# Causal masks in attention on 64 by 64 cells of the array, each product writing one half of the rows

## What is computed

```python
scores = jnp.einsum('bthd,bshd->bhts', q, k) * scale
causal = jnp.tril(jnp.ones((S, S), dtype=bool))
scores = jnp.where(causal[None, None, :, :], scores, -jnp.inf)
probs = jax.nn.softmax(scores, axis=-1)
attended = jnp.einsum('bhts,bshd->bthd', probs, v).reshape(B, S, hidden)
return attended @ Wo.T + bo
```

## Time and profile before

| | |
|---|---|
| median of three runs | 1914.78 us |
| profiled execution | 1914.01 us |
| its span, first to last instruction | 1912.2 us |
| mean granted clock of TensorE, share of 2.4 GHz | 0.907 |
| busy: TensorE, VectorE, ScalarE, GpSimd | 87%, 62%, 49%, 27% of the span |
| MATMUL records | 13482 |

### The profile page before, as it was taken

How to read it: one execution, slowest core, us unless ns; L and a number is a source line. 1 busy time by engine, 2 the same in 40 slices (tenths; PEclk the granted TensorE clock), 3 DMA queues, 4 the chain that set the end, 5 groups by cost and what they waited for, 6 DMA issues and landing times. The chain is left out here.

```text
span 1912.2 us, 33758 instructions
## 1 busy us (share of the span) xinstructions
PE 1656.3 (87%) x13482; PEld 1086.1 (57%) x13482; DVE 1178.0 (62%) x1827; ACT 942.1 (49%) x1898; POOL 517.0 (27%) x401
## 2 busy tenths in 40 slices
PE   2665999999999979999956269999999997999998
PEld 2442455554554568888844235554545445888887
DVE  3545778878785366444464167778878816654444
ACT  1110487777778524334321006777777782444333
POOL 1114166556657512223222110000000000223222
PEclk7775799999999989999978657999999998999999
DMA  4331211112110060000006511020100004100000
GB/s 131 97 105 50 67 50 52 60 50 71 53 43 32 24 264 1 1 1 0 0 21 204 194 48 41 24 68 24 46 30 18 2 2 196 69 12 1 11 11 11
DMA packets 75992, 104.39 MB, mean 55 GB/s; under 512 B 28560, under 2 KB 46736, under 8 KB 75600
## 3 DMA queue, kind: packets, MB, share of 16 engines
q1 hardware_dynamic: 71888, 86.11, 14.0%
q0 software_dynamic: 3968, 16.39, 2.2%
HBM read 61.84 MB, written 40.37 MB: 53 GB/s over the span
## 5 line engine op out<-in xcount | busy, mean ns | idle before, releaser
L974 DVE TENSOR_REDUCE chunk_max<-ring 128x2 f32<-128x1024 f32 (+3 forms) x640 | 670.9, 1064 | 209.3 <-PE ring L881 104.5
L954 ACT ACTIVATE probs<-ps_s 128x512 f32<-128x512 f32 (+3 forms) x1280 | 620.0, 534 | 238.4 <-PE ps_s L911 153.5
L881 PE MATMUL ring<-kt,qt 63*128 63x512 f32 (+3 forms) x1280 | 465.1, 473 | 83.0 <-PEq L408 58.1
L906 PE MATMUL ps_s<-qt,kt 64*128 64x512 f32 (+3 forms) x1280 | 471.3, 437 | 5.2 <-ACT probs L954 4.5
L1245 POOL TENSOR_TENSOR inter_lo<-inter,inter_hi 128x512 fp32r<-128x512 f32 x128 | 165.5, 1293 | 936.3 <-ACT inter_hi L1179 936.3
L923 PE MATMUL ps_o<-probs,vg 128*32 128x256 f32 (+1 forms) x4608 | 360.5, 385 | 0.0
L906 PEld LDWEIGHTS ps_s<-qt,kt 64*128 64x128 f32 x1280 | 214.2, 190 | 239.1 <-ACT probs L954 204.6
L881 PEld LDWEIGHTS ring<-kt,qt 63*128 63x128 f32 x1280 | 206.5, 201 | 118.0 <-issue 59.2
L1219 DVE SCALAR_TENSOR_TENSOR gelu_a<-gelu_a,ps_g 128x512 f32<-128x512 f32 x128 | 88.0, 688 | 183.3 <-ACT gelu_a L1173 183.0
L1173 ACT ACTIVATE gelu_a<-ps_g 128x512 f32<-128x512 f32 x128 | 76.5, 598 | 228.8 <-PE ps_u L94 228.5
L92 PE MATMUL ps_d<-w_mlp,inter_lo 128*128 128x256 f32 x512 | 151.2, 295 | 28.8 <-DVE x L1210 15.2
(11 more groups left out here) (141 smaller groups left out, 2435.8 us busy)
## 6 DMA issues: line engine op xcount, KB each, us to landing
w_mlp<-w_scr SPq DMA_DIRECT2D x32, 768.0 KB, 15.3
w_scr<-w_parts POOLq DMA_DIRECT2D x16, 768.0 KB, 3.6
qt<-q_scr SPq DMA_DIRECT2D x116, 96.0 KB, 2.4
q_scr<-qk_hi SPq DMA_DIRECT2D x32, 256.0 KB
kt<-k_scr SPq DMA_DIRECT2D x80, 96.0 KB, 2.5
q_scr<-qk_lo SPq DMA_DIRECT2D x16, 256.0 KB
v_scr_b<-v_out SPq DMA_DIRECT2D x8, 512.0 KB, 10.3
k_scr<-qk_hi SPq DMA_DIRECT2D x16, 256.0 KB
```

The lines of the kernel that those rows point to most:

```text
L881: op = pe.matmul(out[:, h, 0:w], qt[g][plain[h], p, q0:q0 + P], kt[g][plain[h], p % NKP, c * TW:c * TW + w], start=True, stop=c < t)
L906: op = pe.matmul(out[:, 0:TW - w0], kt[g][shifted[h % 2], (h // 2) % NKP, kb * P:(kb + 1) * P], qt[g][shifted[h % 2], h // 2, t * TW + w0: ...
L954: act.activation(pr[n % NPR][:, h, w0:TW], src[:, 0:TW - w0], ACT.Exp, scale=SCALE).then_inc(s_e, 1)
L974: dve.tensor_reduce(mp[t % 2][:, qb, 2 * p:2 * p + 2, c], ring[n % 2][:, :, 0:w], AX.X, ALU.max).then_inc(s_rd, 1)
```

## The change

Each masking product is cut to the half of the output that it is about. Its weights are the 64 by 64 identity (`ident[half, 0, 0:64]`) for both a; the output is partitions 0 to 63 for a = 0 and 64 to 127 for a = 1; and of the 128 columns only those that can hold a masked value are written: from 64 a on above the diagonal, up to 64 (a + 1) below it. All else stays: the plan, the mask tiles, the semaphores.

```diff
                     if c == t:
                         for a in range(2):
-                            op = pe.matmul(out[:, h, w - P:w], ident[half[h], a, :], above[half[h], a, :],
-                                           start=False, stop=a == 1)
+                            c0 = HALF * a
+                            op = pe.matmul(out[half[a], h, w - P + c0:w], ident[half[h], 0, 0:HALF], above[half[h], a, c0:P],
+                                           start=False, stop=True)
...
                     if diagonal:
                         for a in range(2):
-                            op = pe.matmul(out[:, 0:P], ident[half[h % 2], a, :], below[half[h % 2], a, :],
-                                           start=False, stop=a == 1)
+                            c1 = HALF * (a + 1)
+                            op = pe.matmul(out[half[a], 0:c1], ident[half[h % 2], 0, 0:HALF], below[half[h % 2], a, 0:c1],
+                                           start=False, stop=True)
```

## The result

The changed kernel takes 2593.45 us (median of 4 runs, 2577.16 to 2608.27) against 1917.16 us before (4 runs on the same chip, 1914.37 to 1921.19): a ratio of 1.3523, 95% interval 1.3422 to 1.3625. It is slower by 676 us. The forecast was 2742 us with a range of 2010 to 2950. The profiled execution took 2603.55 us, its span 2601.7 us.

A forecast was written before the change was run, and what follows sets the result against it. TensorE was taken to bound the kernel in attention. Profiled execution 1914.0 us + 360 for waits at shape changes + 468 for the lower clock = 2742 us; its own range 2450 to 2950, overall range 2010 to 2950.

The forecast's parts named there:

- The wait: At each change between 64x128 and 64x64 cells in attention, the array runs empty: 0.095 us, bounds 0 to 0.095.
- All-masked stages: Between PV groups, stages with both scores and both maxima products masked: 2.28 us against some 0.85, 53 us per layer.
- main block: One score or maxima product with its exposed load, stream and wait: 0.435 us at 512 columns, 0.35 at 320.
- masked-S stage: Between PV groups, a stage with both scores S masked: 1.80 us against 0.78, 50 stages, 51 us per layer.
- mask block: One pair of masks: load 0.055, stream 0.07 and wait 0.095, together 0.22 us.
- my table: Sum over the attention stages by which products are masked: 180 us per layer, 360 for both, clock unchanged.
- The clock: TensorE falls to 1.2 GHz over 60% of attention, changed stages 1.6 times as long: 234 us per layer, 468 both.
- the dip of the earlier trace: Ground for the low clock: granted clock 0.50 at 1276.3, at a tile's change where the stream thins out.
- That the clock holds: Rival: in attention the waits come but the clock stays; 2274 us, say 2200 to 2400; chance 0.12.
- That there is no wait: Rival: no wait between 64x128 and 64x64 cells, pairs save 24 us; 1891 us, bounds 1842 to 1914; chance 0.15.
- only the mask's own half waits: Rival: M of the other row half keeps streaming, +0.11 us per pair, 113 us; 2027 us; chance 0.11.

The follow-up runs named there:

- held back: The changed kernel's 64x64 masks, kept in a list and issued together ahead of the next PV or a product that must not pass them: 1920.13 us.
- half in 64x64: The changed kernel, but only the a = 0 masking product has 64x64 cells, a = 1 stays 64x128, all bf16: 2624.66 us.
- M alone: Kernel before, with only the masks of the maxima products M cut to 64x64 cells, those of the scores S as before: 2025.32 us.
- S alone: Kernel before, with only the masks of the scores S cut to 64x64 cells, those of the maxima products M as before: 2429.53 us.
- its own control in 64x128 cells: Kernel before, with masks issued together ahead of PV, in 64x128 cells with only the needed columns: 1896.55 us, ratio 0.9896.

## Why the prediction was right, and where its sizes were off

**The bound.** TensorE was what a microsecond in attention would be paid in, and it was: 676 us more, VectorE's and ScalarE's instructions no longer than before and both waiting for TensorE.

**The wait.** Right, and shown: from a main product to its mask there are 0.42 and 0.43 us, and 0.31 behind an S whose load had been hidden (0.31 or more was asked for); the product behind the masks comes 0.17 after them (0.15 or more), and no load goes ahead of a change. That the price hangs on the changes was confirmed by the runs that altered their number and kept the products (held back; half in 64x64), and by the one that kept 64-column weights and half-height output and lost the wait (float32r). All-masked stages at 2.4 GHz take 2.05 us (S of 512 columns, M of 128) to 2.40 (all of 512), around the 2.3 that was asked for.

**The sizes of the blocks.** A main block of 512 columns was put at 0.435 us and is 0.42 (1532.34 less 1531.92). The masked-S stage was put at 1.80 and is 1.86, with S at 512 columns. The mask block was put at 0.22 and is 0.17. This is the step that failed in size: "mask load (0.055), mask stream 0.07, wait 0.095" is too much by 0.05 us; which of the three is smaller the traces do not separate. Over 1024 pairs this alone is some 50 us. With 0.17 and the measured main blocks my table gives some 150 us per layer for the predicted 180. Another way is to count the stretches at 1.2 GHz (557 of 816 and 607 of 822 us) back to 2.4 GHz by 1.66, which lies between a stage's 1.63 and PV's 1.77, and those of before (59 of 487 and 70 of 469 us) likewise: the phases at full speed then grow from 463 to 595 and from 441 to 581 us. So the waits are 132 + 140 = 272 us by this count and some 300 by the table, for the predicted 360. The count hangs on its factor: with 1.60 or 1.77 in place of 1.66 it gives 294 or 232 us, and the clock gets the rest.

**The clock.** Direction and share were right, and so was the place: of the stages with all four masked 53 ran wholly at 1.2 GHz and 5 wholly at 2.4, of the plain ones 21 and 116. By the same count 336 of 595 and 366 of 581 us of work, 56 and 63%, run at 1.2 GHz, where 60% was taken. So was the factor: a main block with its masks takes 0.72 + 0.24 = 0.96 us at 1.2 GHz for 0.59 at 2.4, 1.63 times where 1.6 was taken:

```profile
1524.29 0.79 PE L907 MATMUL ps_s<-qt,kt 64*128 64x512 f32 x1
1524.29 0.79 PE L881 MATMUL ring<-kt,qt 63*128 63x512 f32 x1
1525.01 0.31 PE L886 MATMUL ring<-mask_above,half_ident 64*64 64x128 bf16 x2
1525.25 0.79 PE L907 MATMUL ps_s<-qt,kt 64*128 64x512 f32 x1
```

PV is 1.77 times as in the earlier trace rows (1.01 for 0.57 us). The low clock costs 221 + 241 = 462 us, almost the predicted 468. But the kernel before had lost 23 + 28 = 51 us of that already, in the openings of the earlier trace rows, and I had not taken them off. The difference is 411. With the 272 of the waits that is 683, the 682 by which the phases grew (it must be near, since both come from one count). Against the forecast the waits were 88 and the clock 57 too high, 145 of the 149 us by which it missed; how the miss divides between the two is as uncertain as the factor.

One of the grounds for the low clock was weaker than it looked. The 1.2 GHz of the openings had begun before them, in stretches in which TensorE did next to nothing (the kernel before):

```profile
139.60:159.00 19.40, 0.23 (x2) 0.27 (x2) 0.00 (x0) 0.00 (x0) 1.00 (x2) 0.50 0.46 139
...
1071.40:1107.00 35.60, 0.00 (x0) 0.00 (x0) 2.14 (x4) 1.19 (x2) 7.56 (x14) 0.50 0.56 175
```

So the openings show a clock that did not rise, not one that fell. That the clock falls with a stream thinned by changes of shape rested on the dip of the earlier trace rows; the changed kernel's diagonal blocks are what shows it.

The count also says in which part M alone and S alone together fall short of the whole change. M alone ran 80 of 539 and 67 of 518 us at 1.2 GHz, S alone 449 of 738 and 467 of 730. By it the waits are 94 and 199 us, 293 together beside the 272; the clock is 8 and 313, 321 together beside the 411. The waits nearly add up, the clock's part does not.

**The rivals.** That the clock holds (2274) fell: 0.67 and 0.64 in the long stretches. It did hold for M alone, with half the pairs. That there is no wait (1891) fell with the first stage of the timeline. That only the mask's own half waits (2027) fell too: M of 128 columns would have let its mask start after some 0.26 us (0.11 load, 0.06 stream, 0.095 wait), and it starts after 0.42, with the S of the other half; and the masked-M stage takes 1.18 to 1.20 us at every width of M. M alone came to 2025 us, near that rival's price for the whole change, by another mechanism: agreement of a total shows nothing.

**What stays open.** Why the clock holds at 0.96 with 512 pairs at M and falls to 0.71 with 512 at S isn't settled. The timeline shows that a masked S costs more (1.86 us for a stage against 1.18, since M no longer lies beside S), so the stream is thinner; no run varied that alone.

## What to carry to other kernels

Before a small product is cut to a smaller cell, look at what stands on either side of it in TensorE's order. Between 64x128 cells and bf16 products of 64x64 cells the whole array waited here, both row halves of it (0.42 us from a main product to its mask, 0.17 from there to the next), and the work side by side that stopped cost far more than the saved columns gave (6 us). If the small shape is wanted, gather its products at a place where the shape changes anyway (here ahead of PV), or cut columns and rows and leave the cells as they are. And when TensorE gets less dense, price its clock as well as its waits: here it was some 390 to 450 of 682 us, by the factor that is taken for it.

## What the runs showed that had not been expected

- 512 pairs changed at M cost 111 us at a clock of 0.96, as many at S 515 us at 0.71.
- Grouping takes all of it back but 5 us (24 beside its own control in 64x128 cells): the four masks of a stage in 64x64 cells start together, and cost 0.17 us ahead of a PV.
- float32r weights of 64 columns between 64x128 products cost next to no wait (idle of 1.4 us ahead of 512 loads; bf16 147.2 us). This was one of two outcomes named beforehand.
- 127-column bf16 weights load in 150 ns for 104, and the kernel with them was no slower: 1903.93 against 1909.34 us on one chip, ratios 0.9843 against 0.9896 on two.
